# Decoder block on one core: attention denominators by features, reciprocals taken there, and both heads of a pair in one score product

## What is computed

```
q = relu(q) + 1e-6;  k = relu(k) + 1e-6
kv    = cumsum(einsum('bhld,bhle->bhlde', k, v), axis=2)
k_cum = cumsum(k, axis=2)
num   = einsum('bhld,bhlde->bhle', q, kv)
den   = maximum(einsum('bhld,bhld->bhl', q, k_cum), 1e-6)
out   = num / den
x = x + out @ out_w.T + out_b
```

## Time and profile before

| | |
|---|---|
| runs | 504.0, 504.06, 502.84 us, median 504.0 |
| the profiled execution | 503.13 us, of which the span of its instructions is 501.3 us |
| mean granted TensorE clock | 0.96 of full speed |
| busy | PE 84%, DVE 60%, POOL 50%, ACT 37% |
| the steps | from about 44 to 360 us; the rest is start and tail |
| a usual step | 9.82 us; steps with `i % 4 == 0` 10.58 us (an extra DVE operation, line 1077) |

### The profile page before, as it was taken

How to read it: one execution, slowest core, us unless ns; L and a number is a source line. 1 busy time by engine, 2 the same in 40 slices (tenths; PEclk the granted TensorE clock), 3 DMA queues, 4 the chain that set the end, 5 groups by cost and what they waited for, 6 DMA issues and landing times. The chain is left out here.

```text
span 501.3 us, 12391 instructions
## 1 busy us (share of the span) xinstructions
PE 422.7 (84%) x4397; PEld 290.3 (58%) x4397; DVE 299.1 (60%) x955; ACT 187.5 (37%) x460; POOL 252.5 (50%) x381
## 2 busy tenths in 40 slices
PE   0898899999998999999999899888689597759960
PEld 0365676776676766676766666666545245536630
DVE  1245666676766676677577576654356266937551
ACT  2262454454453454454355244324344133121200
POOL 3133646644664466446645654755466746531336
PEclk9999999999999999999999999988799799979995
DMA  7931570000000000000000000000002211241142
GB/s 247 336 93 40 158 224 15 12 13 20 16 13 12 22 12 14 12 23 12 13 12 22 13 13 22 12 14 12 12 22 66 70 43 44 73 167 44 43 157 84
DMA packets 27172, 28.26 MB, mean 56 GB/s; under 512 B 3531, under 2 KB 25928, under 8 KB 27112
## 3 DMA queue, kind: packets, MB, share of 16 engines
q1 hardware_dynamic: 24536, 22.27, 13.9%
q0 software_dynamic: 1312, 3.88, 2.7%
q10 hardware_dynamic: 1264, 1.32, 0.7%
HBM read 15.15 MB, written 12.32 MB: 55 GB/s over the span
## 5 line engine op out<-in xcount | busy, mean ns | idle before, releaser
L1434 POOL TENSOR_TENSOR s_t<-s_t,causal 128x512 f32<-128x512 f32 x64 | 80.1, 1273 | 130.4 <-ACT s_t L799 130.4
L1055 DVE TENSOR_TENSOR s_t<-sbank,causal 128x512 f32<-128x512 f32 x64 | 41.2, 686 | 22.5 <-PE sbank L434 22.5
L412 PE MATMUL bank<-h1t,w_qkv 128*128 128x512 f32 x112 | 52.7, 593 | 0.0
L799 ACT ACTIVATE s_t<-sbank 128x512 f32<-128x512 f32 x64 | 34.7, 595 | 24.4 <-PE sbank L434 24.4
L419 PE MATMUL bank<-w_qkv,h1t 128*128 128x256 f32 x128 | 36.6, 409 | 6.3 <-DVE arena L995 6.3
L855 ACT ACTIVATE prob<-sc,nmx 128x77 f32<-128x77 f32 x32 | 11.5, 360 | 75.0 <-DVE nmx L1102 75.0
L538 PE MATMUL bank<-w_out,attn_t 128*128 128x256 f32 x128 | 37.6, 418 | 1.4 <-DVE attn_t L1108 1.1
L434 PE MATMUL sbank<-arena 32*128 32x128 f32 x1024 | 37.5, 283 | 0.0
L434 PEld LDWEIGHTS sbank<-arena 32*128 32x128 f32 x1024 | 31.4, 186 | 10.1 <-issue 10.1
L462 PE MATMUL bank<-s_t,vp 128*32 128x128 f32 x1024 | 35.7, 281 | 1.3 <-POOL s_t L1434 1.3
L400 PE MATMUL bank<-ident,h 128*128 128x128 f32 x128 | 23.8, 299 | 14.4 <-ACT h L806 13.3
(11 more groups left out here) (213 smaller groups left out, 897.2 us busy)
## 6 DMA issues: line engine op xcount, KB each, us to landing
x<-in_x SPq DMA_DIRECT2D x8, 512.0 KB, 7.3
rows<-x SPq DMA_DIRECT2D x32, 128.0 KB, 1.7
out<-x SPq DMA_DIRECT2D x8, 512.0 KB
we<-in_we SPq DMA_DIRECT2D x1, 2048.0 KB
rows<-zeros SPq DMA_DIRECT2D x1, 1408.0 KB, 8.0
xmask<-in_mask POOLq DMA_DIRECT2D x2, 616.0 KB, 6.5
we<-in_we SPq DMA_DIRECT2D x1, 1024.0 KB
arena<-rows SPq DMA_DIRECT2D x2, 512.0 KB, 4.4
```

What stands on the lines that cost most here:

```text
L412: mm = pe.matmul(dst[:, :], w_qkv[:, ch, cb * P:(cb + 1) * P], h1t[:, g % 3, ch, :], start=(ch == 0), stop=(ch == CH - 1))
L799: return act.activation(dst, src, ACT.Copy)
L1055: dve.tensor_tensor(s_t[:, r, :, :], sbank[r][:, :].rearrange("p (s q) -> p s q", s=4), causal[:, :].unsqueeze(1).to_broadcast([P, 4, P]), ...
L1434: pool.tensor_tensor(s_t[:, r, :, :], s_t[:, r, :, :], causal[:, :].unsqueeze(1).to_broadcast([P, 4, P]), ALU.mult)\
```

## The change

The denominators are made with features on partitions from the start. A constant 128x128 table `same_head` (1 where two features belong to one head) is the weights, and `qkc` of each chunk is streamed by it: each feature's row gets the sum over its own head, 128 columns per chunk, in columns 0 to 255 of `bank[2]`. DVE takes the reciprocal of the 128x256 tile there and writes `rden_t` directly. It raises `den_ready`, which now takes the place of `rdt_ready`. The maximum with 1e-6 becomes a minimum with 1e6 on the reciprocal, in the instruction that multiplies the numerators. The small maximum, the small reciprocal, both ACT copies (`rdx`, `rden_t`) and the two PE transposes are gone.

In `scores` the two parities of a chunk go in one product: 256 columns (two planes of `qpar`, 512 columns apart) for each chunk and strip, 8 in all.

```
 scores:
-                    for par in range(2):
-                        for r in range(RG):
-                            rows = slice(32 * r, 32 * r + 32)
-                            col = (2 * ch + par) * P
-                            mm = pe.matmul(sbank[r][:, col:col + P], kt(slot, ch)[rows, tok(t)],
-                                           qpar(slot, ch, par)[rows, tok(t)], start=True, stop=True)
+                    for r in range(RG):
+                        rows = slice(32 * r, 32 * r + 32)
+                        both = sbank[r][:, 2 * ch * P:2 * (ch + 1) * P].rearrange("p (s n) -> p s n", s=2)
+                        mm = pe.matmul(both, kt(slot, ch)[rows, tok(t)], qpair(slot, ch)[rows, :, tok(t)],
+                                       start=True, stop=True)
 PE step:
                     wait(pe, x1_ready, i - 1)
+                    wait(pe, v_ready, i + 1)
                     qk_block(g, i % GT, bank[0])
                 if is_tile(K):
                     wait(pe, qkc_ready, 2 * (K // GT) + 2)
-                    wait(pe, rdt_ready, K)
+                    wait(pe, den_ready, K)
+                    wait(pe, state_ready, 2 * updates(K))
                     for ch in range(CH):
-                        mm = pe.matmul(bank[2][:, ch * HC:(ch + 1) * HC], qkc((K // GT) % 2, ch)[:, tok(K)], head8[:, :],
-                                       start=(ch == 0), stop=(ch == CH - 1), skip_group_check=True)
+                        mm = pe.matmul(bank[2][:, ch * P:(ch + 1) * P], same_head[:, :], qkc((K // GT) % 2, ch)[:, tok(K)],
+                                       start=True, stop=True, skip_group_check=True)
                     mm.then_inc(den_done, 1)
...
-                if is_tile(K):
-                    wait(pe, rdx_ready, K + 1)
-                    wait(pe, state_ready, 2 * (updates(K) + ((K + 1) % TPB != 0)))
-                    for ch in range(CH):
-                        mm = transpose(bank[2][:, ch * P:(ch + 1) * P], rdx[:, ch * P:(ch + 1) * P])
-                    mm.then_inc(rdt_done, 1)
 ACT step:
-                if is_tile(K):
-                    wait(act, rden_ready, K + 1)
-                    wait(act, rdt_done, K)
-                    copy(rdx[:, :].rearrange("p (h e) -> p h e", e=HD),
-                         rden[:, K % 2, :].unsqueeze(2).to_broadcast([P, NH, HD])).then_inc(rdx_ready, 1)
-                    wait(act, rdt_done, K + 1)
-                    wait(act, attn_ready, K - 1)
-                    copy(rden_t[:, K % 2, :], bank[2][:, 0:D]).then_inc(rdt_ready, 1)
 DVE step:
                     wait(dve, den_done, K + 1)
-                    wait(dve, rden_ready, K)
-                    dve.tensor_scalar(den[:, :], bank[2][:, 0:NH], EPS, None, ALU.max).then_inc(den_ready, 1)
+                    wait(dve, attn_ready, K - 1)
+                    dve.reciprocal(rden_t[:, K % 2, :], bank[2][:, 0:D]).then_inc(den_ready, 1)
                 if is_tile(V):
                     v_evict(V)
-                if is_tile(K):
-                    wait(dve, den_ready, K + 1)
-                    wait(dve, rdx_ready, K - 1)
-                    dve.reciprocal(rden[:, K % 2, :], den[:, :]).then_inc(rden_ready, 1)
...
                 if is_tile(M):
                     wait(dve, num_done, M + 1)
-                    wait(dve, rdt_ready, M + 1)
+                    wait(dve, den_ready, M + 1)
                     wait(dve, out_done, M - 1)
-                    dve.tensor_tensor(attn_t[:, M % 2, :, :].rearrange("p c n -> p (c n)"), bank[3][:, 0:D],
-                                      rden_t[:, M % 2, :], ALU.mult).then_inc(attn_ready, 1)
+                    dve.scalar_tensor_tensor(out=attn_t[:, M % 2, :, :].rearrange("p c n -> p (c n)"),
+                                             in0=rden_t[:, M % 2, :], scalar=1.0 / EPS, in1=bank[3][:, 0:D],
+                                             op0=ALU.min, op1=ALU.mult).then_inc(attn_ready, 1)
```

More of the change, by code:

```diff
@@ L63, in decoder_block @@
         own_wide = sb("own_wide", [P, HC * HV])
-        head8 = sb("head8", [P, HC])
+        same_head = sb("same_head", [P, P])
         parity = sb("parity", [P, 2])
@@ L130, in decoder_block @@
         state = sb("state", [P, 3, CH, 2, HD])
-        den = sb("den", [P, NH])
-        rden = sb("rden", [P, 2, NH])
-        rdx = sb("rdx", [P, D])
         rden_t = sb("rden_t", [P, 2, D])
@@ L155, in qpar, with qpair @@
             return arena[:, slot, k * GW:(k + 1) * GW]
+        def qpair(slot, ch):
+            k = 2 * CH + 2 * ch
+            return arena[:, slot, k * GW:(k + 2) * GW].rearrange("p (s n) -> p s n", s=2)
         def ksum(slot, ch):
@@ L254, in decoder_block @@
         (t1_done, qk_done, v_done, s_done, ktr_done, st_done, t2_done, sc_done, num_done, den_done, ptr_done,
-         rdt_done, out_done, px_done, prep_pe, t3_done, x1_done, x12_done, ztr_done, y_done) = (
+         out_done, px_done, prep_pe, t3_done, x1_done, x12_done, ztr_done, y_done) = (
             sem(f"pe_{n}") for n in ("t1", "qk", "v", "s", "ktr", "st", "t2", "xscore", "num", "den", "ptr",
[L257 to L260, removed]
+                                     "out", "px", "prep", "t3", "x1", "x12", "ztr", "y"))
+        (s_copied, h1_ready, h1t_ready, ktok_ready, qpar_ready, h2t_ready, exp_done, pt_ready,
+         prep_act, h3_ready, h3t_ready, hx_ready, th_ready) = (
+            sem(f"act_{n}") for n in ("s", "h1", "h1t", "ktok", "qpar", "h2t", "exp", "pt",
                                       "prep", "h3", "h3t", "hx", "th"))
         (x1_ready, x2_ready, stat_done, mv_ready, s_masked, qk_ready, qkc_ready, ksum_ready, state_ready,
-         v_ready, max_done, nmx_ready, attn_ready, den_ready, rden_ready, rsum_done, xmask_ready, prep_dve,
+         v_ready, max_done, nmx_ready, attn_ready, den_ready, rsum_done, xmask_ready, prep_dve,
          init_dve, first_stat, mv_first_ready, u_ready, z_ready, zstat_done, zmv_ready, out_ready) = (
             sem(f"dve_{n}") for n in ("x1", "x2", "stat", "mv", "s_masked", "qk", "qkc", "ksum", "state",
-                                      "v", "max", "nmx", "attn", "den", "rden", "rsum", "xmask", "prep",
+                                      "v", "max", "nmx", "attn", "den", "rsum", "xmask", "prep",
                                       "init", "first_stat", "mv_first", "u", "z", "zstat", "zmv", "out"))
@@ L650, in y_products @@
                     wait(pe, x1_ready, NT)
-                    wait(pe, rdt_ready, NT)
+                    wait(pe, den_ready, NT)
                     wait(pe, pt_ready, NT)
@@ L1370, in _ @@
             dve.tensor_copy(ident16[:, :], ident[:, :]).then_inc(init_dve, 1)
-            dve.tensor_copy(head8[:, :], own_wide[:, :].rearrange("p (h v) -> p h v", h=HC)[:, :, HD])\
+            own = own_wide[:, :].rearrange("p (h v) -> p h v", h=HC)[:, :, HD:HV]
+            dve.tensor_copy(same_head[:, :].rearrange("p (h e) -> p h e", e=HD), own.to_broadcast([P, HC, HD]))\
                 .then_inc(init_dve, 1)
```

## The result

The changed kernel took 509.35 to 510.57 us in four runs, median 509.84, beside 503.48 for four runs of the kernel before: the ratio is 1.013, interval 1.011 to 1.015. It is slower, as forecast, by 6.4 us where 11.7 were forecast; 515.7 us had been predicted, within 507 to 528. Its profiled execution has a span of 507.5 us where the one before had 501.3.

The account below looks back on a forecast made before the run. PE was taken as the longer thread from the values to the step's end, DVE's 1.14 us hole as the only free cover. Usual steps +0.45, together +11.7 us on the 504.0 median: 515.7 us, range 507 to 528.

Parts of the forecast that it names:

- The mechanism: PE's state product waits for DVE's wide reciprocal, +0.65 us a usual step, and PE's later work queues behind it.
- forecast for them 0.04: Score products on PE, joined to 256 columns: 0.04 us a step won, with bounds of 0 and 0.3.
- the transposes' 0.22: Two PE transposes of the spread reciprocals, at the end of PE's thread: all 0.22 us comes off a step.
- the forecast sign: In the changed profile, an idle bracket of about 0.65 us before the state product, ended by the reciprocal.
- The reciprocal's length: DVE's 128x256 reciprocal: 1.79 us at 6.4 ns a column, from the rows of 1 and 36 columns.
- Rival B: DVE's wide reciprocal is steeper, 8 ns a column, 2.14 us: 525.5 us in all; chance 0.12.
- the sum: Usual step +0.65 - 0.22 + 0.06 (two-operation multiplication) - 0.04 = +0.45 us; over all steps +11.7 us.
- rival C: PE's new idle time brings half-clock stretches, up to 1.7 us each, 527.6 us; chance 0.11, alone or with steeper reciprocal.
- Steps 7, 15 and 23: Without a state product these and step 31 win 0.2 us each, less a little for value eviction: -0.6 together.
- A: Wide reciprocal streams like an ordinary operation, 0.48 us, hidden in DVE's gap: 0.20 a step won, 497.6 us; chance 0.06.
- D: PE's score group shrinks to half of 1.17 us, instructions being the limit: 16 won, 499.7 us; chance 0.02.
- E: DVE's reciprocal just fits, 1.25 to 1.45 us: between 501 and 506 us; chance 0.05.

Follow-up runs that it names:

- experiment 8: Kernel before with a head table of 128 columns, so the denominators' product streams 128 columns a pass; 502.2 us, ratio 0.999.
- experiment 3: Changed kernel with a reciprocal of only the first 128 of the 256 columns, the others left out; 491.4 us, ratio 0.978.
- experiments 7, 9 and 10: Kernel before with two, one and three extra PE products of 512 columns ahead of step 0; 503.1 (ratio 1.003), 504.4 and 504.0 us, last two run once.
- experiment 5: Changed kernel with the state product moved on PE behind the numerators and DVE's state update behind the multiplication; 483.6 us, ratio 0.961.
- experiment 4: Changed kernel with a plain copy of the 128x256 denominators in place of the reciprocal, no division done; 493.3 us, ratio 0.981.
- experiments 1 and 2: Changed kernel with the 16 score products of 128 columns put back, 509.2 us, ratio 1.014; kernel before with only the scores joined, 502.5 us, ratio 1.000.

## Why the prediction was right, and where its size was off

**The mechanism held in each step.** The state product waits for the reciprocal (forecast +0.65 us, measured 6.24 - 5.62 = +0.62 into the step, in which the 0.03 of the scores are already taken off; forecast for them 0.04); the transposes' 0.22 come off. ACT's copies cost nothing, and neither does the denominators' product, though it grew from 0.44 to 0.54 us up to the next product's start: the wait covers it, as forecast, and experiment 8 shows 0.09 where nothing does. From experiment 3 the point from which the reciprocal costs time is 1.19 us, with the gap that the earlier trace rows had shown as 1.14. The idle bracket in front of the state product is 0.49 and not about 0.65, as the forecast sign had it: the 0.65 was the shift of its start, while before it began 0.07 ahead of the values' end, and the values themselves begin 0.06 later.

**The reciprocal's length** was forecast as 1.79 us from the one-column and 36-column rows; it is 1.75. The measured 948 and 1748 ns make 6.25 ns a column, so the slope of the small instructions (6.4) carried nearly unchanged to the large ones. Rival B (8 ns a column) is wrong. The Trainium skill's repeat count of 8 ("VectorE: DVE Perf Modes", the walkthrough of the pipeline), read as eight cycles a column, would have given an estimate of 2.28 us: the trace, with 1.75, disagrees with that reading, and the measurement decides.

**Where 11.7 became 6.2** (profile against profile). Usual steps gained 0.40 and not 0.45, since the multiplication as an instruction of two operations cost nothing (421 ns; the sum had +0.06 from a row of 483): with a little from steps 2 and 3 some 1.3 us over 22 steps. Step 0 became 0.6 us shorter instead of 0.45 longer, 1.0 in all: with no numerators yet, the old spread of `rdx` had held PE for 0.86 us before the transposes, a wait that went with them and that the sum overlooked (second row below). It is the one term, apart from the clock, that came out with the other sign. Steps 29 and 31 lost their half-clock stretches, 2 x 1.3 = 2.6, and the prediction had treated the clock only as something to lose (rival C, which did not come: no stretch at half clock from the first step to 361.9 us). No mechanism of the change is shown for this part, so it may be chance; without it the profile's 6.2 would have been 8.8, nearer the forecast. The first step began 0.4 earlier, which no part of the change explains; it is of the size by which executions differ there, since in experiments 7, 9 and 10, whose code is the same up to that point, the products ahead of the first step begin at 28.6, 27.9 and 27.2 us (28.5 before, 28.0 after). That makes 5.3 of the 5.5; the rest is spread over steps of 0.1. Of the time line of step 0 before, the first PE row and that of the transposes of `rdx`:

```profile
41.25 0.41 PE L400 MATMUL bank<-ident,h 128*128 128x128 f32 x2 [1.04 <-DVE w_3c L1140]
...
46.48 0.44 PE L400 MATMUL bank<-ident,rdx 128*128 128x128 f32 x2 [0.86 <-ACT rdx L799]
```

**Steps 7, 15 and 23**, without a state product, won 0.16 us each, about what was forecast for them. They gave the hint for experiment 5: in the changed kernel itself they already took 9.20. The prediction used them as a term and did not see in them the remedy.

**Rivals.** A needs a reciprocal under 1.19 us; experiment 4 has an instruction of 0.42 in its place, and it is faster than before, as A said (9.66 a step against 9.82, where A had 0.20 a step). D is refuted by experiments 1 and 2. E had its edge at 1.45 us, 0.3 short of what was measured.

## What to carry to other kernels

Before an instruction is moved into an engine's idle gap, compare its length with the gap and then look who waits for its result by way of a shared buffer: here the first 1.19 us were free and the 0.56 beyond were paid in full in nearly every step, not through DVE's own work but through one small PE product queued at the wrong place. Moving the waiter behind work that does not need the result was worth more (1.0 us a step, of which 0.46 can be had without the change) than the change itself had cost (0.4). Widening a reciprocal to save a spread and a transpose trades cheap columns for ones that cost four times as much, so in this kernel it pays only under cover.

## What the runs showed that I had not expected

A reciprocal costs 6.25 ns a column from 128 to 256 columns (948 and 1748 ns), and a copy of 256 columns 415 ns. A two-operation instruction with a constant scalar took 421 ns for 256 columns, as the one-operation one does; another with a scalar read from a tile took 483. Joining two products of 128 columns into one of 256 on a 32-row strip saves 0.02 us on a group of 32 passes. And in profiles of kernels with the same steps 28 to 31 (before, experiments 7, 9 and 10) there were two, two, one and no half-clock stretches in them, worth 1.3 us each, as much as many an edit: before a difference of 2 or 3 us between two profiles is put down to a change, the granted clock of the two is to be read beside it.
